# Layer two's edge sums held in three PSUM banks over a whole block, copied out by ScalarE instead of added by VectorE

## What is computed

```python
def _gat_layer(x, src, dst, W, b, a, g, beta, N, concat):
    h = x @ W.T + b
    s_src = h @ a[:d]
    s_dst = h @ a[d:]
    score = s_src[src] + s_dst[dst]
    e = jnp.exp(-jax.nn.leaky_relu(score, ALPHA))
    h_prime = jax.ops.segment_sum(e[:, None] * h[dst], src, num_segments=N)
    ...
    return jax.nn.elu(h_prime) if concat else h_prime
...
x = jnp.concatenate([_gat_layer(...) for i in range(H)], axis=1)   # 8 heads of 64
out = _gat_layer(x, ..., W_out, ...)                               # 256 wide
...
out = tokens
for e in range(E):
    h = jax.nn.gelu(tokens @ w1[e] + b1[e], approximate=False)
    y = h @ w2[e] + b2[e]
    out = out + combine[:, e:e + 1] * y
```

## Time and profile before

| | us |
|---|---|
| median of three runs | 6240.78 |
| lowest, highest run | 6229.96, 6252.61 |
| span of the profiled execution | 6307.1 |
| layer one, first to last copy (L1229) | 1162.6 to 3710.7 |
| layer two, first to last gather (L1355) | 3732.7 to 6207.5 |

### The profile page before, as it was taken

One profiled execution on the slowest core, in us unless ns is written; L12 is line 12 of the kernel. 1 busy time (PEld: TensorE's weight loads), 2 busy tenths in 40 slices (PEclk: granted clock), 3 DMA queues, 4 the chain that ended last, 5 costly groups with the idle time before them and its releaser, 6 DMA issues. The chain is left out here.

```text
span 6307.1 us, 92011 instructions
## 1 busy us (share of the span) xinstructions
PE 5072.2 (80%) x20985; PEld 2888.8 (46%) x20985; DVE 4560.9 (72%) x15618; ACT 2608.9 (41%) x6620; POOL 3934.9 (62%) x4400
## 2 busy tenths in 40 slices
PE   7878888788888888788888856787888887887888
PEld 4533333333333333333333324666666666666666
DVE  6699999666766666677767655776777777776775
ACT  2278888244544444455454430222222222222223
POOL 2379997466666666666666646666666666666662
PEclk8999999799998999999999876888988888888889
DMA  2200000567777766777777754444444444444441
GB/s 72 63 6 1 1 1 1 158 198 198 199 201 197 198 198 195 199 201 202 202 198 201 198 148 118 115 116 119 118 116 117 114 120 118 116 119 115 119 117 46
DMA packets 323700, 826.45 MB, mean 131 GB/s; under 512 B 73309, under 2 KB 103311, under 8 KB 323187
## 3 DMA queue, kind: packets, MB, share of 16 engines
q0 software_dynamic: 212992, 664.75, 38.5%
q1 hardware_dynamic: 107907, 155.02, 8.5%
q10 hardware_dynamic: 2288, 0.79, 0.1%
HBM read 793.97 MB, written 26.33 MB: 130 GB/s over the span
## 5 line engine op out<-in xcount | busy, mean ns | idle before, releaser
L1106 POOL DMA_INDIRECT heads_rows<-table,shared_node_of x1664 | 1576.0, 947 | 1021.3 <-issue 401.0
L1355 POOL DMA_INDIRECT out_rows<-table,shared_node_of x1664 | 1590.2, 956 | 934.1 <-issue 460.9
L1286 PE MATMUL heads_banks<-heads_rows,heads_hot 128*128 128x512 f32 x3328 | 1914.9, 693 | 176.5 <-DVE heads_rows L1162 89.1
L1229 ACT ACTIVATE sums<-heads_banks x1664 | 973.5, 600 | 1286.7 <-PE heads_banks L1286 838.3
L1502 PE MATMUL out_banks<-out_rows,out_hot 128*128 128x256 f32 x3328 | 1148.8, 437 | 352.4 <-DVE late_sums L1407 257.9
L1162 DVE TENSOR_TENSOR heads_rows<-heads_rows,heads_ps_k 128x512 f32<-128x512 f32 x1664 | 1129.3, 679 | 1.4
L1407 DVE TENSOR_TENSOR late_sums<-out_banks,late_sums 128x256 f32 x1664 | 701.7, 422 | 509.8 <-PE out_banks L1502 184.3
L1502 PEld LDWEIGHTS out_banks<-out_rows,out_hot 128*128 128x128 f32 x3328 | 692.6, 217 | 580.5 <-DVE late_sums L1407 359.5
L1286 PEld LDWEIGHTS heads_banks<-heads_rows,heads_hot 128*128 128x128 f32 x3328 | 545.9, 206 | 511.0 <-issue 481.6
L571 POOL TENSOR_SCALAR sort_plain_lane<-sort_lanes_h,sort_place 125x128 f16<-125x128 f16 x990 | 677.4, 695 | 83.2 <-ACT sort_by_lane L864 52.7
L1462 ACT ACTIVATE out_weight<-out_score 128x4 f32<-128x4 f32 x416 | 85.0, 205 | 1359.0 <-DVE out_score L1389 848.1
(11 more groups left out here) (340 smaller groups left out, 6360.5 us busy)
## 6 DMA issues: line engine op xcount, KB each, us to landing
heads_lanes<-lane_rows SPq DMA_DIRECT2D x208, 256.0 KB
out_lanes<-lane_rows SPq DMA_DIRECT2D x208, 256.0 KB
heads_rows<-table,shared_node_of POOLq DMA_INDIRECT x1664
out_rows<-table,shared_node_of POOLq DMA_INDIRECT x1664
table<-proj_rows SPq DMA_DIRECT2D x50, 227.5 KB
table<-mid_rows SPq DMA_DIRECT2D x50, 113.8 KB
sort_member<-in_x SPq DMA_DIRECT2D x5, 1120.0 KB
moe_x_raw<-in_x SPq DMA_DIRECT2D x50, 112.0 KB
```

The source lines that it names most:

```text
L1106: nc.gpsimd.indirect_dma_start(out=rows[:, g % RING, j, :], out_offset=None, in_=table[:, :], in_offset=bass.IndirectOffsetOnAxis(ap=node_ ...
L1229: nc.scalar.activation(sums_of[:, bass.ds(place * width, width)], banks[:, bass.ds(bank, width)], ACT.Copy)\
L1286: nc.tensor.matmul(banks[:, bass.ds(info[j], width)], hot[:, g % HOTS, j, :], rows[:, g % RING, j, 0:width], start=False, stop=True, skip_ ...
L1355: nc.gpsimd.indirect_dma_start(out=rows[:, g % RING, j, :], out_offset=None, in_=table[:, :], in_offset=bass.IndirectOffsetOnAxis(ap=node_ ...
```

## The change

*Layer two.* A block's steps now add up in PSUM (`start=False`), in bank (block mod 3) of three, each 512 words apart. The bank's number is loaded into a register, four words to a group, on TensorE. ScalarE gets a new piece, `take`: it loads two single words (bank and place), waits for the products, copies the 256 values of the bank to a place in `sums2`, waits for its own copy, and writes zeros into the bank. In the first 38 groups (`ALONE`, 152 steps) there is a take after every step, and TensorE may be three steps ahead of the takes. From group 38 on there is one take after each group: it takes the block that ended in the group, or copies the bank to the last block's place, which the last take overwrites, if none ended. There TensorE enters group g after the take of group g-2. That makes 152 + 378 = 530 takes. VectorE's 1664 additions, its register loads and the memset of `sums2` are gone; in their place stands one memset of the three banks. The experts wait for `takes_by(done_by(rank))` takes. On ScalarE the exponentials of group g+2 stand first, then the experts' pieces, then the group's take.

*Sort.* Two more rows of numbers are made (a step's bank in layer two, the bank of a take), by division by three with rounding, and one of places for the takes from group 38 on.

*Layer one.* `NOWHERES` is 1, and the one place is that of block 49, so each copy waits for the one right before it.

```diff
-NOWHERES = 2
+OUT_BANKS, OUT_BACK = 3, 2
+NOWHERES = 1
+ALONE = -(-3 * BLOCKS // GROUP)
...
+        third = later(1, 2, FP32)[0:1, :, 0:STEPS]
-        nowhere = k["iota"][0:1, BLOCKS:BLOCKS + NOWHERES].unsqueeze(1).unsqueeze(1)\
+        nowhere = k["iota"][0:1, BLOCKS - NOWHERES:BLOCKS].unsqueeze(1).unsqueeze(1)\
...
+                seq.mark(nc.vector.tensor_scalar(third[:, 0, :], blocks, 1.0 / OUT_BANKS, MAGIC, ALU.mult, ALU.add))
+                yield
+                seq.mark(nc.vector.tensor_scalar(third[:, 1, :], before_i, 1.0 / OUT_BANKS, MAGIC, ALU.mult, ALU.add))
+                yield
+                seq.wait()
+                for row in range(2):
+                    seq.mark(nc.vector.tensor_scalar(third[:, row, :], third[:, row, :], -MAGIC, -float(OUT_BANKS), ALU.add, ALU.mult))
+                    yield
+                seq.wait()
+                seq.mark(nc.vector.scalar_tensor_tensor(third[:, 0, :], blocks, 1.0, third[:, 0, :], ALU.add, ALU.add))
+                yield
+                seq.mark(nc.vector.scalar_tensor_tensor(third[:, 1, :], before_i, 1.0, third[:, 1, :], ALU.add, ALU.add))
+                yield
+                seq.wait()
+                for row, kept_at in ((0, 96), (1, 0)):
+                    seq.mark(nc.vector.tensor_scalar(step_info[kept_at:kept_at + 1, STEPS:2 * STEPS], third[:, row, :], 512.0, None, ALU.mult))
+                    yield
...
+                yield
+                firsts, nexts = by_group(blocks)[:, :, 0], by_group(block_row[:, 1 + GROUP:STEPS + 1])[:, :, 0]
+                ended, taken_to = flags[:, 0, 0:GROUPS], flags[:, 0, GROUPS:2 * GROUPS]
+                seq.mark(nc.vector.tensor_tensor(ended[:, 0:GROUPS - 1], firsts[:, 0:GROUPS - 1], nexts, ALU.not_equal))
+                seq.mark(nc.vector.memset(ended[:, GROUPS - 1:GROUPS], 1.0))
+                yield
+                seq.wait()
+                seq.mark(nc.vector.scalar_tensor_tensor(taken_to, firsts, 1.0 - BLOCKS, ended, ALU.add, ALU.mult))
+                yield
+                seq.wait()
+                seq.mark(nc.vector.tensor_scalar(numbers_of(32)[:, ALONE:GROUPS, 1, 0], taken_to[:, ALONE:GROUPS], BLOCKS - 1.0, None, ALU.add))
...
+def takes_by(step):
+
+    return min(step, ALONE * GROUP) + max(0, -(-step // GROUP) - ALONE)
...
-        banks = st.ps("banks", [P, BANKS, HALVES, FEAT])
+        banks = st.ps("banks", [P, OUT_BANKS * 512])
...
-            def add_bank(run):
-                for step in range(run * HALVES, (run + 1) * HALVES):
-                    if step % (BATCH * GROUP) == 0:
-                        places["now"] = block_ids(mybir.EngineType.DVE, step // GROUP)
-                    place = places["now"][step % (BATCH * GROUP)]
-                    if step % HALVES == 0:
-                        dve.wait_ge(s["summed"], base["summed"] + (run + 1) * HALVES)
-                    if step:
-                        dve.wait_ge(s["taken"], base["taken"] + step)
-                    here = sums_of[:, bass.ds(place * FEAT, FEAT)]
-                    nc.vector.tensor_tensor(here, banks[:, run % BANKS, step % HALVES, :], here, ALU.add).then_inc(s["taken"], 1)
+            nc.vector.memset(banks[:, :], 0.0).then_inc(s["zeroed"], 1)
...
-            nc.vector.memset(sums_of[:, :], 0.0).then_inc(s["zeroed"], 1)
-            dve.wait_ge(s["zeroed"], base["zeroed"] + 1)
...
-                if ADDED_LATE <= g * HALVES < STEPS // HALVES + ADDED_LATE:
-                    add_bank(g * HALVES - ADDED_LATE)
...
-                if ADDED_LATE <= g * HALVES + 1 < STEPS // HALVES + ADDED_LATE:
-                    add_bank(g * HALVES + 1 - ADDED_LATE)
...
+            def words(row, at, most):
+                _, (value,) = nc.values_load_multi_w_load_instructions(
+                    step_info[row:row + 1, at:at + 1], engines=(mybir.EngineType.Activation,), min_val=0, max_val=most,
+                return nc.s_assert_within(value, 0, most, skip_runtime_bounds_check_because="a bank or a block")
+
+            def take(bank_at, place_at, summed, takes):
+                bank = words(0, STEPS + bank_at, (OUT_BANKS - 1) * 512)
+                place = words(32, place_at, BLOCKS - 1)
+                here = banks[:, bass.ds(bank, FEAT)]
+                act.wait_ge(s["summed"], base["summed"] + summed)
+                if takes:
+
+                    act.wait_ge(emptied, takes)
+                nc.scalar.activation(sums_of[:, bass.ds(place * FEAT, FEAT)], here, ACT.Copy).then_inc(s["taken"], 1)
+                act.wait_ge(s["taken"], base["taken"] + takes + 1)
+                nc.scalar.activation(here, k["iota"][:, 0:1].to_broadcast([P, FEAT]), ACT.Copy, scale=0.0).then_inc(emptied, 1)
+
             for g in range(GROUPS):
-                extra.upto(g * GROUP)
                 if g + AHEAD < GROUPS:
                     make_weight(g + AHEAD)
                 extra.upto(g * GROUP + GROUP - 1)
+                if g < ALONE:
+                    for j in range(GROUP):
+                        step = g * GROUP + j
+                        take(step, g * 2 * GROUP + GROUP + j, step + 1, step)
+                else:
+                    take(g * GROUP + GROUP - 1, g * 2 * GROUP + GROUP, (g + 1) * GROUP, takes_by(g * GROUP))
...
+            pe.wait_ge(s["zeroed"], base["zeroed"] + 1)
             for g in range(GROUPS):
+                _, here = nc.values_load_multi_w_load_instructions(
+                    step_info[96:97, STEPS + g * GROUP:STEPS + (g + 1) * GROUP], engines=(mybir.EngineType.PE,), min_val=0,
+                    max_val=(OUT_BANKS - 1) * 512, skip_runtime_bounds_check_because="the sort writes them within bounds")
+                if g >= ALONE:
+                    pe.wait_ge(emptied, takes_by((g if g < ALONE + OUT_BACK + 1 else g - OUT_BACK + 1) * GROUP))
                 for j in range(GROUP):
-                    step, run = g * GROUP + j, (g * GROUP + j) // HALVES
-                    if step % HALVES == 0 and run >= BANKS:
-
-                        pe.wait_ge(s["taken"], base["taken"] + (run - BANKS + 1) * HALVES)
+                    step = g * GROUP + j
+                    if g < ALONE and step >= OUT_BANKS:
+
+                        pe.wait_ge(emptied, step - OUT_BANKS + 1)
                     pe.wait_ge(s["ready"], base["ready"] + step + 1)
-                    nc.tensor.matmul(banks[:, run % BANKS, step % HALVES, :], hot[:, g % HOTS, j, :], rows[:, g % RING, j, 0:FEAT],
-                                     start=True, stop=True).then_inc(s["summed"], 1)
+                    nc.tensor.matmul(banks[:, bass.ds(here[j], FEAT)], hot[:, g % HOTS, j, :], rows[:, g % RING, j, 0:FEAT],
+                                     start=False, stop=True, skip_group_check=True).then_inc(s["summed"], 1)
...
-            dve.wait_ge(taken, EACH_TURN["taken"] + done_by(rank))
+            dve.wait_ge(taken, EACH_TURN["taken"] + takes_by(done_by(rank)))
...
-            sums1 = heads.enter_context(nc.sbuf_tensor("sums1", [P, (BLOCKS + NOWHERES) * HD], FP32))
+            sums1 = heads.enter_context(nc.sbuf_tensor("sums1", [P, BLOCKS * HD], FP32))
```

29 lines of the change are left out of this document (12 added, 17 removed).

## The result

The changed kernel takes 6276.5 us (four runs, 6264.4 to 6287.0), the kernel before 6244.0 (6230.0 to 6252.6) beside it: a ratio of 1.0057, 95% interval 1.004 to 1.0074. In a second comparison it was 6274.7 (six runs) against 6240.6, 1.0045 (1.0029 to 1.0062). One of those six took 6406.9 us at a granted clock of 0.71, and without it their median is 6273.1. So the change costs 33 us. The sum had said -8, within what can't be told from no change.

A forecast was written before the change was run, and what follows sets the result against it. The prediction took GpSimd's gathers, 1.25 us each plus pauses on late signals, to bound layer two. Terms 6 + 12 - 5 + 15 - 36 summed to -8 us, so 6233 us in the median's terms; range 6130 to 6320.

The forecast's parts named there:

- the row with 4.46 us: Layer two's timeline: VectorE stands 4.46 us ahead of an addition with its input complete, read as signals about 4 us late.
- Rival B2: Layer two: occupancy is the bound, TensorE alone would set the pace, -270 us, 5970 us; chance 0.05.
- Steady part, -36 forecast: Layer two, steps 152 to 1663: with VectorE less loaded, 1.468 us a gather, 1512 x 0.024 = -36 us.
- A: The whole sum as forecast, -8 us, range 6185 to 6275 us, with 1.468 us a gather in layer two; chance 0.50.
- Rival B: Layer two: late signals were VectorE's own, so gather streams grow, 1.43 us a step, -94 us, 6155 us; chance 0.22.
- First 152 steps, +15 forecast: Start of layer two: three steps of credit over late signals make GpSimd stop oftener, 1.57 us a step, +15 us (0 to +60).
- Rival C: ScalarE's take is the longer chain: +45 steady, +35 first 152 steps, +15 layer one, 6335 us; chance 0.21.
- Layer one, +12 forecast: Layer one: copies' waits for an earlier copy double from 37.6 us and a third reaches TensorE, +12 us (0 to +50).
- Sort, +6 forecast: Sort loop: 11.4 us of added VectorE operations, some 5 us covered by waits, +6 us (+3 to +11.4).
- Start of layer two, -5 forecast: Ahead of layer two's first product: clearing takes 1.3 us, not 10.72, so it starts earlier, -5 us (-10.7 to 0).
- TensorE's loads: Layer two: a four-word register load a group, 0.28 us each, 19 us of TensorE's time where the gathers set the pace.
- End, 0 forecast: After the steps: last products, the last blocks' experts and the output keep their order, 0 us.

The follow-up runs named there:

- alone0_b: The changed kernel with ALONE = 0, one take a group from the start of layer two: 6239.2 us, ratio 0.9995 to the kernel before.
- before_b: The kernel before, unchanged, run again for a second profile: 6241.8 us, ratio 1.0013 to before.
- credit8: The changed kernel with TensorE allowed eight steps ahead of the takes, not three, in the first 38 groups: 6271.6 us, ratio 1.0053 to before.
- both0_b: The changed kernel with ALONE = 0 and NOWHERES = 2 as before: 6236.5 us, ratio 1.0002 to the kernel before.

## Why the prediction was wrong, by its own steps

*What bounds the kernel.* That the gathers hold layer two, and not VectorE's or TensorE's busy time, was right; the runs without gathers show it (-482 us for before). My reading of the row with 4.46 us was loose: by the order of the queue the addition at 3859.99 is the second of its pair, which waits for VectorE's own last addition alone and not for a product. And by ScalarE's loads of 0.70 us, what I called late signals can be, at least in part, a queue that goes slowly.

Rival B2 took TensorE for the bound, by the rule of the Trainium skill on the engine with the highest occupancy ("Perfetto Trace Analysis", Identifying the Most-Contended Engine). TensorE's work stayed as it was, so the unchanged pace alone says nothing against it. The same work done faster does: 1.26 us a step in the prompt condition and 1.04 without gathers. I had also set that rule against VectorE's 71%, which wasn't the highest share; 549 us less of VectorE in 2165 changed nothing.

*Steady part, -36 forecast, 0 measured.* This is the step that gave the wrong sign. I set 1.492 us a gather against 1.468 from an earlier stretch of the same profile with VectorE less busy, and took the difference for what slack on the engines gives. The level of 1.492 was a property of that execution: another profile of before has 1.471. The inference failed as well. The second profile is faster early too, 1.452 us a gather from the 48th to the 152nd, but so is `alone0_b`, 1.445 there and 1.472 in the steady part, though VectorE is busy 46% of its steady part and no longer 72%. So the early stretch isn't faster through VectorE's slack; through what stays open. The pace of 1.468 that I had named as the sign of A came out (1.471) with nothing gained. The profile's span, 66 us above the median, was noted and then carried over as if it changed no difference.

Nor did GpSimd's waits for the ring shrink with VectorE's work. The waits ahead of gathers were 294.6 us for TensorE and 142.0 "remote" in `before_b`,

```profile
  PE out_banks L1502: 294.6, 231
  remote: 142.0, 68
```

and in `alone0_b`

```profile
  PE out_banks L1545: 250.9, 202
  remote: 183.0, 93
```

437 and 434 us: the same total, whoever is named. Rival B, with its 1.43 us a step, falls. What this shows is the exchange as a whole; no run took the additions away without putting takes in their place.

*First 152 steps, +15 forecast (0 to +60), +34 by medians and +37 by profiles.* The place was right, the size and the cause were not. I took ScalarE's take for 1.15 us plus a handshake and held that this lay below 1.47; I blamed the three steps of credit. `credit8` left the cost at 35 us (6271.6 against 6236.4). A register load of one word took 0.279 us, not 0.1 (the row below: least, median, most), the copy 0.384 and the clearing 0.387, not 0.467. The two errors nearly cancel, at 1.22 us a take; the four durations add up to 1.33, so a part of the loads runs beside the clearing. What was missed is the sum for the group: four takes, the exponential and the experts' pieces in one queue, with 1.0 us a group left to catch up after the stretches in which that queue goes slowly.

```profile
L1483 ACTq TENSOR_LOAD <-shared_step_info x1060: 4/279/718, 3722.4 to 6200.9; - x177
```

Rival C named this: the take as the longer chain, with the weights behind it, +35 in the first 152 steps. Its other two terms (+45 in the steady part, +15 in layer one) were 0. Without the -36 my own sum would have been +28, near the 33 measured, but by luck: +12 of it, for layer one, wasn't there, and the +15 was 34 to 37.

The formula of the Trainium skill for an activation with immediate scale and bias ("ScalarE: Activation LUTs", What ACT_TABLE_LOAD costs) gives 0.399 us for 256 elements, an estimate from that page; the rows have 0.384 and 0.387.

*Layer one, +12 forecast, 0 measured.* The copies' own waits rose, though they didn't double, from 34.1 us in 84 (`before_b`) to 55.9 in 212 in the first profile of the changed kernel (49.4 in 200 in the second):

```profile
  ACT sums L1265: 55.9, 212
```

None of it shows at the end: 1529 gathers in the 2300 us, 1524 before, and by the ratios `both0_b` with two places (1.0002) is no faster than `alone0_b` with one (0.9995).

*Sort, +6 forecast.* The first gather of layer one starts at 1147.3 and 1149.5 us after, and at 1144.0 and 1145.0 before: +2 to +5 us. In the prompt condition it is 1145.2 to 1149.9 with the longer sort and 1139.7 to 1142.4 without. *Start of layer two, -5 forecast:* from the last gather of layer one to the first of layer two it is 48.4 us (second profile of the changed kernel) and 45.9 (`before_b`), and nothing of a gain shows in the 277 against 278 us of `alone0_b`. *TensorE's loads* of four words took 0.334 us each, and no cost of them shows in the steady part. *End, 0 forecast:* from the last gather to the end it is 100 us in both profiles of before and 92 and 95 in those of the changed kernel, so the one term that I had put at nothing gained 5 to 8 us.

Summed over the second profiles: sort +4.5, layer one -5.4, start +2.5, layer two +36.7 and end -4.8 make +33.5 us, their spans differ by 33.6, and the medians by 33.
